# All transposes of a slot between up and down projection, contexts in the work banks, and the second exponentials of the last pair behind silu

## The chip, the cores and the metric

The kernel runs on one core of one Trainium2 chip. The metric is the device time in microseconds (us) of one execution. PE is TensorE, PEld its weight loads, ACT ScalarE, DVE VectorE, POOL GpSimd and SP SyncE, which issues nearly all DMAs here. A time such as "1479.32" is counted in us from the start of the profiled span.

## The reference, cut to what matters

128 graphs of 128 nodes with 384 features go through one transformer layer, with a final layer norm. The bias `adj` is added to the attention scores of all eight heads (48 features each).

```python
q, k, v = (split_heads(x @ w + b) for w, b in ((wq, bq), (wk, bk), (wv, bv)))
scores = einsum('bhqd,bhkd->bhqk', q, k) * 48 ** -0.5 + adj[:, None]
ctx = merge_heads(einsum('bhij,bhjd->bhid', softmax(scores), v))
x1 = rmsnorm(x + ctx @ wo + bo, alpha1, gamma1)
ff = silu(x1 @ w1 + b1) @ w2 + b2            # 384 -> 1536 -> 384
y = rmsnorm(x1 + ff, alpha2, gamma2)
out = layernorm(x + y)
```

## The kernel before

Two graphs make a pair (`PAIR` = 2, index `b`), so there are 64 pairs `g`, the last being 63. One pass of the outer loop is a slot `t`; there are 67 in use. A slot works on several pairs at once: it projects pair `t` to queries, keys and values, takes scores and softmax of pair `t-1`, context and attention output of pair `t-2`, and the feed-forward of pair `t-3`. From slot 3 to slot 63 all of it is live. Each engine has a program of its own, written out by hand in the order of `slot_program(t)`; engines meet through semaphores only, and a wait holds up everything behind it on its engine.

Every product with weights is made of three fp32r passes: each operand is split into a high part (written by ACT, `transposed_hi`, `context_hi`) and a low part (written by DVE, `transposed_lo`, `context_lo`). Products need their input with features on the partitions, so PE transposes `x` (`transpose_x`: 6 matmuls with the identity), the normalised `x1` (`transpose_x1`: 6) and the probabilities (`transpose_probs`: 8 for each graph). ACT copies the transposed probabilities back to SBUF (`probsT_out`, L657), and `context` (L510 and L514, 32-column tiles of the array) reads the copy.

PSUM is full: `ps_att[0]` and `ps_att[1]` (two banks each) hold scores and transposed probabilities, `ps_rows[0]` and `ps_rows[1]` hold contexts, attention outputs and down projections, and `ps_work[0]` and `ps_work[1]` hold the outputs of query, key, value and up projections in turn. The transposes of x and x1 borrow a work bank and a rows bank.

PE's order in a full slot is: transposes of x(t), of the probabilities of graph 0, of x1(t-3), of the probabilities of graph 1; contexts of graph 0 and 1; scores (L526); output product; query, key and value projections; up (six parts of 18 matmuls, L448, each followed by a silu on ACT, L722, and `split_h` on DVE, L883 and L885); down (L595, 36 matmuls for each graph). The transposes thus stand right before the contexts that read them.

ACT does Exp and Silu from different tables and loads each once a slot (L776 and L784). DVE's order around the softmax is: bias and maximum, `residual1`, `norm1` of both graphs (L873 and L877), `keys_out` (L845), `normalise` and `values_out`. SP issues in a slot, among others, the load of x for the residual, the bias, the next x, ten moves of queries and keys within SBUF (L364), and in slot 2 six loads of weights (L324). The first slots also split weights on ACT (L642) and DVE (L802).

Of the kernel before, what the change touches and what calls it, by code (L numbers as in the profile page):

```python
# [26 lines left out]
def build_layer(nc, x, adj, wq, bq, wk, bk, wv, bv, wo, bo, w1, b1, w2, b2,  # L27
# [17 lines left out]
    with ctx:  # L45
# [232 lines left out]
        def x1_first(g):  # L278

            return ps_work[0][:, 0:2 * toks] if g < last else ps_att[0][:, 0:2 * toks]  # L280

        def x1_third(g):

            return ps_rows[1][:, 0:toks] if g < last else ps_att[0][:, 2 * toks:3 * toks]
# [156 lines left out]
        def _(pe):  # L441
# [17 lines left out]
            def transpose_x(g):  # L459
                pe.wait_ge(x_in_loaded, through(g, 16))  # L460

                if live(g - LAG_FF - 1):
                    pe.wait_ge(silu_ready[fc // 2 - 2], through(g - LAG_FF - 1))
                elif live(g - 1):
                    pe.wait_ge(v_ready[0], through(g - 1))
                transpose_rows(ps_work[1][:, 0:2 * toks], x_in, (0, 1), xT_done[0])

                if live(g - LAG_FF - 1):
                    pe.wait_ge(res2_ready[0], through(g - LAG_FF - 1))
                elif live(g - LAG_ATTN - 1):  # L470
                    pe.wait_ge(res1_ready[0], through(g - LAG_ATTN - 1))
                transpose_rows(ps_rows[0][:, 0:toks], x_in, (2,), xT_done[1])

            def transpose_probs(g, b):
                pe.wait_ge(probs_ready[b], through(g, 2))
                for head in range(HEADS):
                    mm = pe.transpose(ps_att[b][:, head * P:(head + 1) * P], probs[:, b, head, :], ident[:])  # L477
                mm.then_inc(probsT_done[b], 1)

            def transpose_x1(g):  # L480
                for b in range(PAIR):
                    pe.wait_ge(x1_ready[b], through(g))

                if g == last:
                    pe.wait_ge(probsT_ready[0], through(g))
                elif live(g - 1):
                    pe.wait_ge(res2_ready[1], through(g - 1))
                transpose_rows(x1_third(g), x1[:, g % 2], (2,), x1T_done[1])

                if g < last:  # L490
                    if live(g - 1):
                        pe.wait_ge(silu_ready[fc // 2 - 1], through(g - 1))
                    else:
                        pe.wait_ge(v_ready[1], through(g + LAG_FF - 1))
                transpose_rows(x1_first(g), x1[:, g % 2], (0, 1), x1T_done[0])

            def context(g, b):
                pe.wait_ge(probsT_ready[b], through(g))
                pe.wait_ge(v_ready[b], through(g))

                if b == 0 and live(g + LAG_ATTN):
                    pe.wait_ge(xT_lo[1], through(g + LAG_ATTN))
                elif b == 0:
                    pe.wait_ge(res2_ready[0], through(g + LAG_ATTN - LAG_FF - 1))
                elif live(g + LAG_ATTN - LAG_FF):
                    pe.wait_ge(x1T_lo[1], through(g + LAG_ATTN - LAG_FF))
                for side in range(2):
                    for pair in range(hp):
                        head = 2 * pair + side
                        pe.matmul(ps_rows[b][pair * TILE:(pair + 1) * TILE, 2 * P:3 * P], v_rest[:, g % 2, b, head, :],  # L510
                                  probs[:, b, place(head), :], start=(side == 0), stop=(side == 1))
                for head in range(HEADS):
                    p0, at = head % 4 * TILE, head // 4 * P
                    mm = pe.matmul(ps_rows[b][p0:p0 + TILE, at:at + P], v_first[:, g % 2, b, head, :],  # L514
                                   probs[:, b, place(head), :], start=True, stop=True)
                mm.then_inc(ctx_done[b], 1)

            def scores(g, b):
                if b == 0:
                    pe.wait_ge(qk_moved, through(g, 16 * len(moves)))  # L520
                if live(g - 1):
                    pe.wait_ge(probsT_ready[b], through(g - 1))
                for head in range(HEADS):
# [8 lines left out]
            def output_product(g, b):  # L532
                pe.wait_ge(ctx_lo[b], through(g))
# [4 lines left out]
            def project_qk(g):  # L538
                for i in range(2):
                    pe.wait_ge(xT_lo[i], through(g))  # L540
                for n, blocks in enumerate((((wq_s, 0), (wq_s, 1)), ((wq_s, 2), (wk_s, 0)),
# [4 lines left out]
                    if n == 0 and live(g - LAG_FF):  # L546
                        pe.wait_ge(x1T_lo[0], through(g - LAG_FF))
                    elif n == 0 and live(g - 1):
                        pe.wait_ge(v_ready[1], through(g - 1))
                    elif n == 2:  # L550
                        pe.wait_ge(qk_ready[0], through(g))
# [14 lines left out]
            def up(g):  # L566
# [3 lines left out]
                for m in range(fc // 2):  # L570
# [5 lines left out]
                    elif m == 0 or g == last:  # L576
# [22 lines left out]
            def slot_program(t):  # L599
                g_scores, g_attn, g_ff = t - LAG_SCORES, t - LAG_ATTN, t - LAG_FF  # L600
                if live(t):
                    transpose_x(t)
                if live(g_attn):
                    transpose_probs(g_attn, 0)
                if live(g_ff) and g_ff < last:
                    transpose_x1(g_ff)
                if live(g_attn):
                    transpose_probs(g_attn, 1)
# [14 lines left out]
                if live(g_ff):  # L623
# [3 lines left out]
                    if g_ff == last - 1:  # L627
                        transpose_x1(last)
# [8 lines left out]
        def _(act):  # L637
# [22 lines left out]
            def context_hi(g, b):  # L660
                act.wait_ge(ctx_done[b], through(g))
                act.activation(ctxT[:, b, HI].rearrange("p c n -> p (c n)"), ps_rows[b][:, 0:d],
# [65 lines left out]
            def slot_program(t):  # L728
                g_scores, g_attn, g_ff, g_out = t - LAG_SCORES, t - LAG_ATTN, t - LAG_FF, t - LAG_FF - 1
                if t == 0:  # L730
                    weights_hi(t, "queries")
                if live(t):
                    transposed_hi(t, 0, ps_work[1], xT_done, xT, xT_hi)
                    transposed_hi(t, 1, ps_rows[0], xT_done, xT, xT_hi)
                if t == 0:
                    weights_hi(t, "keys")
                    weights_hi(t, "values")
                if live(g_attn):
                    probsT_out(g_attn, 0)
                if live(g_ff) and g_ff < last:  # L740
                    transposed_hi(g_ff, 1, x1_third(g_ff), x1T_done, x1T, x1T_hi)
                if live(g_attn):
                    probsT_out(g_attn, 1)
                    context_hi(g_attn, 0)
                if live(g_ff) and g_ff < last:
                    transposed_hi(g_ff, 0, x1_first(g_ff), x1T_done, x1T, x1T_hi)
                if live(g_attn):
                    context_hi(g_attn, 1)
                if live(g_out):
                    output_squares(g_out, 1)  # L750
                weights_hi(t, "softmax")
# [15 lines left out]
                if live(g_scores):  # L767
# [6 lines left out]
                weights_hi(t, "end")  # L774
                if live(g_ff):
# [4 lines left out]
                    if g_ff == last - 1:  # L780
                        transposed_hi(last, 1, x1_third(last), x1T_done, x1T, x1T_hi)
                        transposed_hi(last, 0, x1_first(last), x1T_done, x1T, x1T_hi)
                    if live(g_scores + 1):
                        act.preload_act_table(ACT.Exp)  # L784
                    output_squares(g_ff, 0)
# [4 lines left out]
        def _(dve):  # L790
# [21 lines left out]
            def context_lo(g, b):  # L812
                dve.wait_ge(ctx_hi[b], through(g))
                dve.tensor_tensor(ctxT[:, b, LO].rearrange("p c n -> p (c n)"), ps_rows[b][:, 0:d],  # L814
# [101 lines left out]
            def slot_program(t):  # L916
# [5 lines left out]
                if live(t):  # L922
                    transposed_lo(t, 0, ps_work[1], xT_hi, xT, xT_lo)
                    transposed_lo(t, 1, ps_rows[0], xT_hi, xT, xT_lo)
                if t == 0:
# [3 lines left out]
                if live(g_ff) and g_ff < last:  # L929
                    transposed_lo(g_ff, 1, x1_third(g_ff), x1T_hi, x1T, x1T_lo)  # L930
                if live(g_attn):
                    context_lo(g_attn, 0)
                if live(g_ff) and g_ff < last:
                    transposed_lo(g_ff, 0, x1_first(g_ff), x1T_hi, x1T, x1T_lo)
                if live(g_attn):
                    context_lo(g_attn, 1)
# [30 lines left out]
                if live(g_scores):  # L967
                    for half in range(2):
                        normalise(g_scores, 1, half)
                weights_lo(t, "end")  # L970
                if live(g_ff):
# [3 lines left out]
                    if g_ff == last - 1:  # L975
                        transposed_lo(last, 1, x1_third(last), x1T_hi, x1T, x1T_lo)
                        transposed_lo(last, 0, x1_first(last), x1T_hi, x1T, x1T_lo)
# [31 lines left out]
```

## Time and profile before

| | |
|---|---|
| time, median of 3 runs | 2948.49 us (2948.18 to 2950.1) |
| the profiled execution | 2949.07 us, its span 2947.3 us |
| granted TensorE clock, mean | 0.997 of full speed |
| PE busy | 2910.8 us, 99% of the span |
| PEld busy | 2857.1 us, 97% |
| DVE, ACT, POOL busy | 63%, 49%, 23% |
| one full slot, from transposes to transposes | 45.43 us |

In the timeline a row is a run of like instructions on one engine: start, length, engine, line, operation, output and input tiles, and count. Matmuls overlap: a row's length runs to the end of its last one, so the pace of matmuls is read from starts. A bracket at the end is idle time of the engine and what ended it.

### The profile page before, as it was taken

What the parts mean: (1) busy time and instruction counts of PE and PEld (TensorE: products, weight loads), DVE (VectorE), ACT (ScalarE), POOL (GpSimd) and SP (SyncE); (2) the same over time, 40 slices, a digit from 0 to 9 for tenths busy, and PEclk for the clock granted to TensorE, in tenths of its full rate; (3) what the DMA queues carried; (4) which work ended last, traced back from release to release, by engine and by line L of the source; (5) the groups of instructions that cost most, each with busy time, mean ns of one, the idle gap of its engine ahead of it and who ended that gap; (6) DMA issues with size and microseconds to landing.
All of it is one profiled execution on the core that took longest, in us unless ns stands there. A gap on an engine that the chain in (4) does not pass through costs nothing.

```text
span 2947.3 us, 62438 instructions
## 1 busy us (share of the span) xinstructions
PE 2910.8 (99%) x25216; PEld 2857.1 (97%) x25216; DVE 1853.1 (63%) x3621; ACT 1443.2 (49%) x4258; POOL 684.8 (23%) x968
## 2 busy tenths in 40 slices
PE   7999999999999999999999999999999999999998
PEld 7999999999999999999999999999999999999998
DVE  6665656657666566566665665656656656566564
ACT  5544545545445455454454554544545445445442
POOL 0122222222222222222222222222221222222222
PEclk9999999999999999999999999999999999999999
DMA  5211212212112121121221211212212112122110
GB/s 164 80 51 53 69 40 64 57 52 64 48 56 69 40 64 56 54 64 44 60 64 46 64 53 52 68 42 62 61 48 64 53 51 69 41 63 60 49 46 28
DMA packets 155489, 171.91 MB, mean 58 GB/s; under 512 B 18624, under 2 KB 155200, under 8 KB 155200
## 3 DMA queue, kind: packets, MB, share of 16 engines
q1 hardware_dynamic: 151952, 166.92, 19.5%
q8 instruction: 199, 3.26, 0.5%
q10 hardware_dynamic: 3248, 0.99, 0.2%
q14 instruction: 90, 0.74, 0.1%
HBM read 92.35 MB, written 25.17 MB: 40 GB/s over the span
## 4 chain that ended last, share of the span: by engine, by line
PE 95%; ACT 3%; DVE 1%; DMA 1%; SPq 1%; issue 0%; POOL 0%; ACTq 0%; POOLq 0%
PE ps_work L448 47%; PE ps_rows L595 28%; PE ps_rows L448 7%; PE ps_att L526 4%; PE ps_att L477 4%; ACT probs L657 2%; PE ps_work L456 2%; PE ps_rows L510 1%; PE ps_rows L514 1%; PE ps_rows L456 1%; SPq L364 0%; DMA x_in<-in_x 0%; ACT probs L668 0%; DVE w_s L802 0%; DMA stage<-in_L_gnn_wq 0%
## 5 line engine op out<-in xcount | busy, mean ns | idle before, releaser
L448 PE MATMUL ps_work<-x1T,w_s 128*128 128x256 f32 x6912 | 823.2, 280 | 3.7 <-ACT h_raw L722 3.7
L448 PEld LDWEIGHTS ps_work<-x1T,w_s 128*128 128x128 f32 x6912 | 820.8, 188 | 3.9 <-ACT h_raw L722 3.9
L595 PE MATMUL ps_rows<-w_s,h 128*128 128x384 f32 x4608 | 824.0, 340 | 0.0
L595 PEld LDWEIGHTS ps_rows<-w_s,h 128*128 128x128 f32 x4608 | 810.6, 188 | 0.0
L722 ACT ACTIVATE h_raw<-ps_work,b_col 128x256 f32<-128x256 f32 x768 | 322.3, 471 | 534.8 <-PE ps_work L448 531.3
L668 ACT ACTIVATE probs<-probs,neg_max 128x128 f32<-128x128 f32 x1024 | 396.4, 390 | 158.2 <-DVE neg_max L827 158.2
L430 POOL TENSOR_TENSOR x<-x,rows 128x768 f32<-128x768 f32 x64 | 117.7, 1840 | 1165.4 <-DVE h L885 1165.4
L883 DVE CAST h<-h_raw 128x512 fp32r<-128x512 f32 x384 | 164.3, 428 | 313.8 <-ACT h_raw L722 313.8
L894 DVE TENSOR_TENSOR y<-ps_rows,x 128x384 f32<-128x384 f32 x128 | 71.4, 558 | 415.0 <-PE ps_rows L595 415.0
L885 DVE TENSOR_TENSOR h<-h_raw,h 128x512 fp32r<-128x512 f32 x384 | 265.9, 692 | 13.2
L697 ACT ACTIVATE squares<-y 128x384 f32<-128x384 f32 x128 | 66.6, 521 | 329.3 <-DVE y L894 329.3
L448 PE MATMUL ps_work<-xT,wq_s 128*128 128x256 f32 x1728 | 216.9, 283 | 2.8 <-DVE xT L809 2.8
L448 PE MATMUL ps_rows<-wo_s,ctxT 128*128 128x384 f32 x1152 | 217.8, 343 | 0.0
L448 PEld LDWEIGHTS ps_work<-xT,wq_s 128*128 128x128 f32 x1728 | 214.5, 191 | 3.4 <-DVE xT L809 3.1
L448 PE MATMUL ps_work<-wv_s,xT 128*128 128x384 f32 x1152 | 211.6, 337 | 4.0 <-DVE qk_flat L845 3.0
L448 PE MATMUL ps_work<-xT,wk_s 128*128 128x256 f32 x1728 | 213.4, 280 | 0.9 <-ACT qk_flat L706 0.9
L448 PEld LDWEIGHTS ps_work<-xT,wk_s 128*128 128x128 f32 x1728 | 207.4, 188 | 1.1 <-ACT qk_flat L706 1.1
L448 PEld LDWEIGHTS ps_rows<-wo_s,ctxT 128*128 128x128 f32 x1152 | 197.3, 188 | 7.9 <-DVE ctxT L814 0.3
L418 POOL TENSOR_TENSOR x_in<-x_in,rows 128x768 f32<-128x768 f32 x64 | 117.0, 1828 | 374.3 <-DMA x_in<-in_x 374.3
L448 PEld LDWEIGHTS ps_work<-wv_s,xT 128*128 128x128 f32 x1152 | 197.6, 188 | 5.0 <-DVE qk_flat L845 3.6
L652 ACT ACTIVATE xT<-ps_work 128x512 fp32r<-128x512 f32 x64 | 38.2, 597 | 333.1 <-PE ps_work L456 333.1
L668 ACT ACTIVATION_READ_ACCUMULATOR probs<-probs,neg_max 128x1 f32 x1024 | 193.1, 189 | 0.0
(87 smaller groups left out, 3576.8 us busy)
## 6 DMA issues: line engine op xcount, KB each, us to landing
x_in<-in_x SPq DMA_DIRECT2D x128, 384.0 KB, 3.1
qk<-qk_flat SPq DMA_DIRECT2D x381, 96.0 KB, 2.3
x_last<-in_x SPq DMA_DIRECT2D x64, 384.0 KB, 3.6
out<-y SPq DMA_DIRECT2D x63, 384.0 KB, 2.7
bias<-in_adj SPq DMA_DIRECT2D x64, 128.0 KB, 2.1
qk<-qk_flat SPq DMA_DIRECT2D x127, 64.0 KB, 2.1
qk<-qk_flat SPq DMA_DIRECT2D x127, 32.0 KB, 2.0
stage<-in_L_gnn_w SPq DMA_DIRECT2D x17, 192.0 KB, 4.0
```

The costliest lines, as they stand in the source:

```text
L418: pool.tensor_tensor(x_in[:], x_in[:], row(BO), ALU.add).then_inc(x_res_biased, 1)
L430: pool.tensor_tensor(x1[:, g_ff % 2], x1[:, g_ff % 2], row(B2), ALU.add).then_inc(x1_b2_ready, 1)
L448: mm = pe.matmul(ps_out, stationary(sta), moving(mov), start=(i == 0), stop=(i == n - 1))
L456: mm = pe.transpose(ps_out[:, at:at + P], rows_in[:, b, kb * P:(kb + 1) * P], ident[:])
L477: mm = pe.transpose(ps_att[b][:, head * P:(head + 1) * P], probs[:, b, head, :], ident[:])
L526: mm = pe.matmul(ps_att[b][:, at:at + P], qk[p0:p0 + dh, Q, c, b * P:(b + 1) * P], qk[p0:p0 + dh, K, c, b * P:(b + 1) * P], start=True, st ...
L595: mm = pe.matmul(ps_rows[b][:, 0:d], h[:, sta, m, b * P:(b + 1) * P], w2_s[:, mov, m, :], start=(m == 0 and i == 0), stop=(m == fc - 1 and ...
L668: e = act.activation(probs[:, b, head, :], probs[:, b, head, :], ACT.Exp, bias=neg_max[:, b, head:head + 1], accum_out=row_sum[:, b, head: ...
L722: e = act.activation(h_raw[:, m % 2, j * toks:(j + 1) * toks], ps_work[(m + 1) % 2][:, j * toks:(j + 1) * toks], ACT.Silu, bias=b1_col[:, ...
L883: dve.tensor_copy(hi, h_raw[:, m % 2, :]).then_inc(h_hi[m], 1)
L885: dve.tensor_tensor(h[:, LO, 2 * m:2 * m + 2, :].rearrange("p c n -> p (c n)"), h_raw[:, m % 2, :], hi.bitcast(F32), ALU.subtract).then_in ...
L894: dve.tensor_tensor(y[:, b, :], ps_rows[b][:, 0:d], x1[:, g % 2, b, :], ALU.add).then_inc(res2_ready[b], 1)
```

## The change

In a full slot PE now begins with both contexts; scores, output product, projections and up follow as before. Between up and down stand all transposes: probabilities of pair `t-1` (both graphs), x of pair `t+1`, x1 of pair `t-2`, each one slot earlier than it was. The contexts lie in `ps_work[0]` and `ps_work[1]`, the transposes of x in `ps_work[1]` and `ps_work[0]`, those of x1 in `ps_att[0]`, behind ACT's copy out of that tile. ACT and DVE have their copies in the matching places, ahead of the Exp table load. On DVE `norm1` of graph 1 moves behind the layer norm of graph 1, that is, from ahead of `keys_out` to behind `values_out`. For the last pair the probabilities are transposed at the start of slot 65, and the exponentials of its graph 1, with their normalisation, come behind the silus and x1 copies of slot 64.

```diff
 PE
-        def x1_first(g): ... ps_work[0] (last pair: ps_att[0])
-        def x1_third(g): ... ps_rows[1] (last pair: ps_att[0])
+        x_banks = (ps_work[1][:, 0:2 * toks], ps_work[0][:, 0:toks])
+        x1_banks = (ps_att[0][:, 0:2 * toks], ps_att[0][:, 2 * toks:3 * toks])
...
             def transpose_x(g):
+                for i, blocks in enumerate(((0, 1), (2,))):
+                    if live(g - LAG_FF - 1):
+                        pe.wait_ge(silu_ready[fc // 2 - 2 + i], through(g - LAG_FF - 1))
+                    elif live(g - 1):
+                        pe.wait_ge(v_ready[i], through(g - 1))
+                    transpose_rows(x_banks[i], x_in, blocks, xT_done[i])
...
             def transpose_x1(g):
+                if g == last - 1:
+                    pe.wait_ge(scores_biased[0], through(last))
+                else:
+                    pe.wait_ge(probsT_ready[0], through(min(g + 1, last)))
...
             def context(g, b):
                 pe.wait_ge(probsT_ready[b], through(g))
                 pe.wait_ge(v_ready[b], through(g))
+                if live(g + LAG_ATTN):
+                    pe.wait_ge(xT_lo[1 - b], through(g + LAG_ATTN))
-                        pe.matmul(ps_rows[b]...
+                        pe.matmul(ps_work[b]...
...
             def scores(g, b):
+                if b == 0 and live(g + LAG_SCORES - LAG_FF):
+                    for i in range(2):
+                        pe.wait_ge(x1T_lo[i], through(g + LAG_SCORES - LAG_FF))
...
             def slot_program(t):
-                transpose_x(t); transpose_probs(g_attn, 0)
-                transpose_x1(g_ff); transpose_probs(g_attn, 1)
+                if g_attn == last:
+                    for b in range(PAIR):
+                        transpose_probs(last, b)
                 context(g_attn, 0 and 1); scores; output_product; projections; up(g_ff)
+                if live(g_scores) and g_scores < last:
+                    for b in range(PAIR):
+                        transpose_probs(g_scores, b)
+                if live(g_ff) and live(t + 1):
+                    transpose_x(t + 1)
+                if live(g_attn):
+                    transpose_x1(g_attn)
                 down(g_ff, 0 and 1)
 ACT
+                if live(g_out):
+                    output_squares(g_out, 1)        # now ahead of the contexts
+                context_hi(g_attn, 0 and 1)
...
-                if live(g_scores):
+                if live(g_scores) and g_scores < last:
                     exponentials(g_scores, 1)
                 silu(g_ff)
+                probsT_out(g_scores, 0 and 1); x_out(); transposed_hi(g_attn, x1 banks)
+                    if live(g_scores + 1) or g_scores == last:
                         act.preload_act_table(ACT.Exp)
+                    if g_scores == last:
+                        exponentials(last, 1)
 DVE
-                    for b in range(PAIR):
-                        norm1(g_attn, b)
+                    norm1(g_attn, 0)
                 keys_out, normalise, values_out, layer_norm(g_out, 1)
+                if live(g_attn):
+                    norm1(g_attn, 1)
```

## Rows read from the trace of the kernel before

**Rows 1.** The page: busy line of the engines, the chain that ended last by line.
```profile
PE 2910.8 (99%) x25216; PEld 2857.1 (97%) x25216; DVE 1853.1 (63%) x3621; ACT 1443.2 (49%) x4258; POOL 684.8 (23%) x968
...
PE ps_work L448 47%; PE ps_rows L595 28%; PE ps_rows L448 7%; PE ps_att L526 4%; PE ps_att L477 4%; ACT probs L657 2%; PE ps_work L456 2%; PE ps_rows L510 1%; PE ps_rows L514 1%; PE ps_rows L456 1%; SPq L364 0%; DMA x_in<-in_x 0%; ACT probs L668 0%; DVE w_s L802 0%; DMA stage<-in_L_gnn_wq 0%
```

**Rows 2.** All waits: who waited for whom, us in total, times, longest.
```profile
PEld ps_rows L510 <- ACT probs L657: 23.7, 64, 0.4
...
PEld ps_rows L510 <- issue: 10.8, 64, 0.2
...
PE ps_work L448 <- ACT h_raw L722: 3.7, 1, 3.7
```

**Rows 3.** Timeline of PE over one full slot.
```profile
1476.17 0.60 PE L456 MATMUL ps_work<-ident,x_in 128*128 128x128 f32 x4
...
1478.35 1.04 PE L477 MATMUL ps_att<-ident,probs 128*128 128x128 f32 x8
1479.32 0.64 PE L510 MATMUL ps_rows<-probs,v_rest 128*32 128x128 f32 x16
1479.78 0.62 PE L514 MATMUL ps_rows<-probs,v_first 128*32 128x128 f32 x16
1480.50 0.65 PE L510 MATMUL ps_rows<-probs,v_rest 128*32 128x128 f32 x16
...
1481.51 2.06 PE L526 MATMUL ps_att<-qk 48*128 48x128 f32 x32
...
1508.88 12.88 PE L595 MATMUL ps_rows<-w_s,h 128*128 128x384 f32 x72
1521.60 0.60 PE L456 MATMUL ps_work<-ident,x_in 128*128 128x128 f32 x4
```

**Rows 4.** Timeline of PE, second half of the matmuls that begin at 1479.78.
```profile
1479.99 0.40 PE L514 MATMUL ps_rows<-probs,v_first 128*32 128x128 f32 x8
```

**Rows 5.** Timeline of ACT in the same slot: copy, sixth silu, table load.
```profile
1479.42 1.02 ACT L657 ACTIVATE probs<-ps_att 128x1024 f32<-128x1024 f32 x1 [0.23 <-PE ps_att L477]
...
1509.08 0.84 ACT L722 ACTIVATE h_raw<-ps_work,b_col 128x256 f32<-128x256 f32 x2 [1.27 <-PE ps_work L448]
1509.94 1.28 ACT L784 ACT_TABLE_LOAD   x1
```

**Rows 6.** Timeline of PE, slot 65: up, transposes, down.
```profile
2900.64 0.82 PE L456 MATMUL ps_att<-ident,x 128*128 128x128 f32 x6
2901.22 12.73 PE L595 MATMUL ps_rows<-w_s,h 128*128 128x384 f32 x72
```

**Rows 7.** Timeline of ACT in slot 3: a weight's copy, then a silu.
```profile
90.99 0.52 ACT L642 ACTIVATE w_s<-stage 128x384 fp32r<-128x384 f32 x1
92.32 0.84 ACT L722 ACTIVATE h_raw<-ps_work,b_col 128x256 f32<-128x256 f32 x2 [0.80 <-PE ps_work L448]
```

**Rows 8.** Timeline of PE in slot 3, second value projection.
```profile
86.23 1.83 PE L448 MATMUL ps_work<-wv_s,xT 128*128 128x384 f32 x9 [1.69 <-DVE qk_flat L845]
```

**Rows 9.** Timeline of DVE in slot 3.
```profile
77.86 0.56 DVE L868 TENSOR_TENSOR x<-ps_rows,x_in 128x384 f32<-128x384 f32 x1 [4.86 <-POOL x_in L418]
...
84.18 0.61 DVE L873 SCALAR_TENSOR_TENSOR x<-x,inv_rms,rows 128x384 f32<-128x384 f32 x1
...
85.30 0.87 DVE L845 TENSOR_SCALAR qk_flat<-ps_work,bk_col 128x256 f32<-128x256 f32 x2
```

**Rows 10.** Timeline of SP, the residual's load of slot 3.
```profile
71.73 0.38 SPq L315 DMA_DIRECT2D x_in<-in_x  x1
```

**Rows 11.** Timeline of slot 64: PE, ACT and DVE.
```profile
2849.09 4.43 PE L448 MATMUL ps_work<-x1T,w_s 128*128 128x256 f32 x36
2857.25 10.32 PE L448 MATMUL ps_work<-x1T,w_s 128*128 128x256 f32 x72 [3.73 <-ACT h_raw L722]
...
2851.78 0.19 ACT L686 ACTIVATION_READ_ACCUMULATOR squares<-x 128x1 f32 x1
...
2857.26 0.48 DVE L913 TENSOR_SCALAR y<-y,mean_var,inv_std 128x384 f32<-128x384 f32 x1
```

More of the change, by code:

```diff
@@ L482, in transpose_x1 @@
                     pe.wait_ge(x1_ready[b], through(g))
[L484 to L495, printed above, removed]
+                if g == last - 1:
+                    pe.wait_ge(scores_biased[0], through(last))
+                else:
+                    pe.wait_ge(probsT_ready[0], through(min(g + 1, last)))
+                for i, blocks in enumerate(((0, 1), (2,))):
+                    transpose_rows(x1_banks[i], x1[:, g % 2], blocks, x1T_done[i])
             def context(g, b):
@@ L499, in context @@
                 pe.wait_ge(v_ready[b], through(g))
[L501 to L506, printed above, removed]
+                if live(g + LAG_ATTN):
+                    pe.wait_ge(xT_lo[1 - b], through(g + LAG_ATTN))
+                else:
+                    pe.wait_ge(silu_ready[fc // 2 - 1 - b], through(g + LAG_ATTN - LAG_FF - 1))
                 for side in range(2):
@@ L544, in project_qk @@
                         pe.wait_ge(weight_split, (n + 1) * kd)
[L546 to L550, printed above, removed]
+                    if n == 2:
                         pe.wait_ge(qk_ready[0], through(g))
@@ L779, in slot_program @@
                     silu(g_ff)
[L780 to L783, printed above, removed]
+                elif live(t + 1):
+                    x_out()
+                weights_hi(t, "end")
+                if live(g_scores) and g_scores < last:
+                    for b in range(PAIR):
+                        probsT_out(g_scores, b)
+                if live(g_ff) and live(t + 1):
+                    x_out()
+                if live(g_attn):
+                    for i in range(2):
+                        transposed_hi(g_attn, i, x1_banks[i], x1T_done, x1T, x1T_hi)
+                if live(g_ff):
+                    if live(g_scores + 1) or g_scores == last:
                         act.preload_act_table(ACT.Exp)
+                    if g_scores == last:
+                        exponentials(last, 1)
                     output_squares(g_ff, 0)
@@ L928, in slot_program @@
                     weights_lo(t, "values")
-                if live(g_ff) and g_ff < last:
-                    transposed_lo(g_ff, 1, x1_third(g_ff), x1T_hi, x1T, x1T_lo)
                 if live(g_attn):
[L932 to L936, printed above, removed]
+                    for b in range(PAIR):
+                        context_lo(g_attn, b)
                     if g_attn == 0:
@@ L966, in slot_program @@
                     layer_norm(g_out, 1)
-                if live(g_scores):
+                if live(g_attn):
+                    norm1(g_attn, 1)
+                if live(g_scores) and g_scores < last:
                     for half in range(2):
                         normalise(g_scores, 1, half)
-                weights_lo(t, "end")
                 if live(g_ff):
@@ L974, in slot_program @@
                         weights_lo(t, m)
-                    if g_ff == last - 1:
-                        transposed_lo(last, 1, x1_third(last), x1T_hi, x1T, x1T_lo)
-                        transposed_lo(last, 0, x1_first(last), x1T_hi, x1T, x1T_lo)
+                if live(t + 1):
+                    for i in range(2):
+                        transposed_lo(t + 1, i, x_banks[i], xT_hi, xT, xT_lo)
+                weights_lo(t, "end")
+                if live(g_attn):
+                    for i in range(2):
+                        transposed_lo(g_attn, i, x1_banks[i], x1T_hi, x1T, x1T_lo)
+                if g_scores == last:
+                    for half in range(2):
+                        normalise(last, 1, half)
+                if live(g_ff):
                     residual2(g_ff, 0)
```

75 lines of the change are left out of this document (27 added, 48 removed).

## The prediction

> **What bounds the kernel now.** I read the page first. PE is busy for 99% of the span, and the chain that ended last is PE nearly throughout; the one other line with a visible share is ACT's copy of the transposed probabilities, L657, with 2% [rows 1]. No other engine can be the bound of a full slot, so what is there to win is PE's idle time and nothing else, and the list of waits says where that lies. Weight loads of the context's first line wait 64 times for ACT's copy, 23.7 us in total, and 64 times for nothing visible, 10.8 us; and there is one long wait of 3.7 us for a silu [rows 2]. Then the timeline of a full slot, for the exact size. Slots repeat every 1521.60 - 1476.17 = 45.43 us [rows 3]. The transposes of graph 1 begin at 1478.35, the copy of them begins 1.07 us later and takes 1.02 us [rows 5], and the context of graph 1 can only start at 1480.50, when that copy has ended [rows 3]. The context of graph 0 fills part of the time, not all.
>
> **The gap in a full slot.** The second half of the context's 16 matmuls at L514 starts at 1479.99 [rows 4], the first at 1479.78 [rows 3], so eight take 0.21 and 16 take 0.43 us. Context 1 could start at 1480.21; it starts at 1480.50, which is 0.29 us lost. It also starts from an idle array: from L510 to L514 it is 0.46 us in a context that begins so [rows 3], against 0.43 at pace, another 0.02 to 0.03. With both contexts at the head of the slot, copies made a down projection earlier (12.72 us, from 1508.88 to 1521.60), this is gone: **0.31 us a slot**.
>
> **The joints.** The change replaces three joints of PE's order (down to transposes, transposes to context, up to down) by three others (up to transposes, transposes to down, down to context). First the pace of transposes: four run 0.60 us and eight 1.04 us from the first start to the last end [rows 3], so one takes 0.11 us at pace and 0.27 us by itself. Up to transposes to down exists already in slot 65: six transposes begin at 2900.64 and down at 2901.22 [rows 6], 0.58 us where six at pace take 0.65; these two joints cost nothing. Down to context is new. Its nearest row is transposes to context: eight transposes and the joint take 0.97 us [rows 3], some 0.09 us above their pace of 0.88. I take the same for down to context, so the joint nets to nothing: the 10.8 us of "issue" ahead of the contexts [rows 2] stay, only behind another neighbour. The bounds of the new joint are 0 (then another 0.09 us a slot is won) and 0.16 us: a matmul of down has a pace of 12.72 / 72 = 0.177 us and the last runs to 1521.76 [rows 3], so it takes 0.34 us by itself, 0.07 more than a transpose; if that is paid in full, 0.07 us a slot is lost.
>
> The Trainium skill, "TensorEngine Tiling (Array Packing)", section Key Properties, says that changing the tiling mode, not just the tile, drains TensorE. By it the context's 32-column tiles must wait for whatever stood before to leave the array. The trace agrees: the passage from transposes into the context shows 0.09 us [rows 3]. By this rule the number of changes of mode is the same before and after, and only the longer matmul ahead speaks against the change.
>
> **What could be late behind the moved transposes.** Call the end of up U. The 16 transposes of probabilities and 6 of x take 22 x 0.109 = 2.4 us (0.109 is the 0.11 above with a digit more, (1.04 - 0.27) / 7), all 28 with those of x1 take 3.05 us. Those of x need the fifth and sixth silu. The sixth ends at 1509.08 + 0.84 = 1509.92, U + 1.04, as up ends at 1508.88 [rows 3, 5]; the block that needs it comes at U + 2.2. Those of x1 go into `ps_att[0]` and wait for ACT's copy of graph 0: the copy may begin at U + 1.07, just when the silu is done, ends at U + 2.10, and PE follows a copy by 0.05 us (1480.44 to 1480.50) [rows 3, 5]: U + 2.15. PE is there at U + 2.40. This is the tightest place of the new order; **it has 0.25 us to spare**. Behind it on PE stands down, so lateness here counts in full. Down needs only its first high and low parts of h, long done, and the sixth only at its eleventh step. ACT then has copies of graph 1, x and x1 (about 3 us) and the table load of 1.28 us [rows 5] until about U + 6, before squares that wait for the first half of down; DVE's four subtractions end near U + 5.5. All that is covered by down.
>
> At the head of the next slot ACT has squares first, then two context copies. Contexts take 1.8 us and scores 2.0 us [rows 3], so the output product starts about 4.0 us after down's end; down's residual, squares and both splits of context 0 end at about 2.5, of context 1 at 3.2, since each is an operation of 384 columns like that at 77.86, 0.56 us [rows 9]. Cost 0; without this cover it would be as much as they come late. DVE's `norm1` of graph 1 (85.30 - 84.18 = 1.12 us [rows 9]) moves behind the value outputs and delays the first split of h by under 1 us, against 1.5 us until the third silu asks for it: cost 0. On SP the residual's load now waits for transposes one slot earlier, so it lands during down; what stands behind it (bias, next x) is not wanted before the middle of the next slot. POOL adds to it behind its work for graph 0 and is done about 0.7 us into the slot, before the root that it owes graph 1. The extra waits before scores and the output product are for things 10 us old.
>
> **How many slots.** Contexts stand in slots 2 to 65. In slots 2 and 3 PE waits for DVE's normalised probabilities or for a DMA right there, so nothing is won; slot 65 is below. Slots 4 to 64 are 61: 61 x 0.31 = **18.9 us**.
>
> **The first slots.** In slot 3 the second value projection waits 1.69 us for `keys_out` [rows 8], which stands behind both `norm1` on DVE. One of them moves away: 1.12 us earlier [rows 9]. The chain ahead of it hangs on the residual's load, issued at 71.73 [rows 10]; in SP's order it stands behind six weight loads and ten moves, which start when `keys_out` of slot 2 is done; that has the same `norm1` ahead of it, so it too is about 1.15 us earlier, and so is DVE's residual at 77.86, which waited 4.86 us for it [rows 9]. Together 1.12 + 1.15 = **2.3 us**, bounds 0 and 2.6. Slots 1 and 2 win and lose a few tenths, since DVE's order ends at the same time; I take 0.
>
> **The last slots.** In slot 64 the third part of up waits for silu. ACT is free of squares at 2851.97 [rows 11] and had the eight exponentials of graph 1 next; without them the table is loaded until 2853.25 and the first silu ends at 2854.1. PE began at 2849.09 and its two parts run 4.43 us to the last end [rows 11], so with 0.17 us of overlap the third could start at 2853.35: 0.8 us idle, and 2.1 us for a part. The third silu then waits for the first split of h, which DVE reaches after its layer norm (2857.26 + 0.4) [rows 11] and has done at 2858.75 (estimated at 1.1 us, as the two operations of `norm1` [rows 9]); the silu ends at 2859.6, and PE, which had the fourth part done at 2858.4, idles 1.25. In all 2.05 us against 3.9 before (from 2853.35 to 2857.25): **1.8 us** won, bounds 1.2 and 3.7. The exponentials end about 8 us behind up, under down. In slot 65 both transposes of probabilities now stand bare ahead of the contexts: 0.31 for the first copy and 0.14 for the second, against 0.31 before: 0.14 lost.
>
> **Sum.** 18.9 + 2.3 + 1.8 - 0.1 = 22.9 us. The profiled execution took 2949.07 (span 2947.3): 2926.2. The median of the runs is 0.6 lower: **2925.6 us**.
>
> **Rivals.**
> 1. *The longer matmul makes down to context dear*, 0.07 us a slot: 61 x 0.07 = 4.3 less, 2929.9. For it: the last matmul of down is longer. Against: it is also longer at pace (0.177 against 0.109). 0.12.
> 2. *Only the full slots win*, because the first slots hang on something else (weights) and slot 64 on DVE: 18.9 alone, 2929.6. For it: DVE and SP are both crowded there. 0.08.
> 3. *The stall moves to the transposes of x1.* If the copy of graph 0 ends 0.25 us later than worked out, PE starts to wait; at 0.25 + 0.31 = 0.56 us the full slots win nothing, and only the ends (4 us) or less remain: 2944 to 2948. For it: ACT has silu and copy back to back. Against: both durations stand in the rows to 0.02 us. 0.05.
> 4. *Slower: the copies stand between Silu and Exp, and each change of function loads a table.* One more load of 1.28 us ahead of the copy at U + 1.07 makes the x1 transposes 1.28 - 0.25 = 1.03 us late. From 0.56 us on it decides the sign. 61 x (1.03 - 0.31) = 44 slower, less 4: 2989. Against it: in slot 3 copies of weights stand between silus, with 0.80 us idle between copy and next silu, and no load [rows 7]. Any other lateness of ACT at this place over 0.56 us belongs here too. 0.07.
>
> The Trainium skill, "ScalarE: Activation LUTs", section Table sets, says that tables are loaded as sets of functions, one load for each change of set. By it a copy could cost a load at this place if it were not in silu's set; in this trace it is.
>
> **How the numbers follow.** Forecast 0.68, rivals 0.12, 0.08, 0.05 and 0.07. Range: up to rivals 1 and 2 with a part of both together, 2933; down, if the new joint costs nothing (61 x 0.09 = 5.5) with 0.5 for the ends: 2920. Forecast alone: 2923 to 2928. No change that can be told is within 0.2%, 5.9 us: 2942.6 to 2954.4. Faster by more: 0.88; within: 0.05; slower: 0.07.
>
> **What would show it.** The L510 wait for ACT's copy should vanish from the list but for slot 65; a slot should take 45.12 us; context 0 should follow down by some 0.27 us from the last matmul's start, and context 1 follow at pace; up should be followed by 28 transposes in 3.05 us without a hole; the value projection of slot 3 should wait under 1 us. A wait of PE at L456 for L657 would be rivals 3 or 4, with an added table load in the latter; a longer hole ahead of L510 rival 1.

## The result, and the profile after

The changed kernel takes 2911.72 us (median of 4 runs, 2910.08 to 2916.1), the one before 2949.3 (4 runs beside it): ratio 0.9876, 95% interval 0.9861 to 0.9891. That is 37.6 us less, where 22.9 were forecast (2925.6) and the range ended at 2920. The direction was right, the size was not.

The page after has a span of 2908.3 us, 39.0 below the 2947.3 of before. Its busy line and its chain answer to [rows 1]:

```profile
PE 2882.5 (99%) x25216; PEld 2841.8 (98%) x25216; DVE 1846.2 (63%) x3621; ACT 1431.3 (49%) x4259; POOL 684.3 (24%) x968
...
PE ps_work L443 48%; PE ps_rows L581 27%; PE ps_rows L443 7%; PE ps_att L514 4%; PE ps_att L470 4%; PE ps_work L495 2%; PE ps_work L499 2%; PE ps_att L451 1%; PE ps_work L451 1%; SPq L359 0%; DMA x_in<-in_x 0%; DVE w_s L802 0%; DMA stage<-in_L_gnn_wq 0%; POOL x_in L413 0%; DVE neg_max L827 0%
```

ACT's copy, 2% of the chain before, is gone from it. But look at PE: the same 25216 matmuls are busy for 2882.5 us instead of 2910.8, 28.3 us less. A closed gap explains part of that, because the profile counts the drain of the last matmul before a gap as busy: of the 0.31 us that the gap cost, 0.10 were idle (1479.78 + 0.62 = 1480.40 to 1480.50 [rows 3]). The other 0.21 in 61 slots are 13 us, less than half of the 28.3. The rest has to lie elsewhere. The waits of the changed kernel (answer to [rows 2]) show the gap closed and the joint left:

```profile
PEld ps_work L495 <- issue: 15.7, 63, 0.3
...
PEld ps_work L495 <- ACT probs L649: 0.8, 2, 0.5
```

And one full slot on PE, which answers to [rows 3] and [rows 6]:

```profile
1459.16 0.64 PE L495 MATMUL ps_work<-probs,v_rest 128*32 128x128 f32 x16
1459.62 0.62 PE L499 MATMUL ps_work<-probs,v_first 128*32 128x128 f32 x16
1460.06 0.62 PE L495 MATMUL ps_work<-probs,v_rest 128*32 128x128 f32 x16
...
1475.75 12.83 PE L443 MATMUL ps_work<-x1T,w_s 128*128 128x256 f32 x108
1488.42 1.91 PE L470 MATMUL ps_att<-ident,probs 128*128 128x128 f32 x16
1490.17 0.82 PE L451 MATMUL ps_work<-ident,x_in 128*128 128x128 f32 x6
1490.82 0.82 PE L451 MATMUL ps_att<-ident,x 128*128 128x128 f32 x6
1491.39 12.73 PE L581 MATMUL ps_rows<-w_s,h 128*128 128x384 f32 x72
1504.06 0.65 PE L495 MATMUL ps_work<-probs,v_rest 128*32 128x128 f32 x16
```

Context 1 follows context 0 after 0.44 us from L499 to L495, at pace; the transposes run without a hole. The slot takes 1504.06 - 1459.16 = 44.90 us against 45.43: 0.53 less, not 0.31. The missing 0.22 is in down. Its 72 matmuls run 12.73 us here and 12.88 before [rows 3], although the one here begins with a slower first step (0.26 us). Ten microseconds from the middle of down, before and then after:

```profile
1509.77 10.41 PE L595 MATMUL ps_rows<-w_s,h 128*128 128x384 f32 x58
```

```profile
1492.69 10.56 PE L581 MATMUL ps_rows<-w_s,h 128*128 128x384 f32 x60
```

A stretch of n matmuls lasts n-1 steps and the 0.34 us of the last one: (10.41 - 0.34) / 57 = 0.1767 us a step before, (10.56 - 0.34) / 59 = 0.1732 after. Over 70 steps that is 0.24 us a slot, in matmuls with the same operands and shapes, all at a granted clock of 1.00. In the slow pace the steps alternate between 0.179 and 0.174 us, in the quick one each is 0.173. The same difference stands already in the rows of before: 12.88 us for down in a usual slot [rows 3], 12.73 in slot 65, where six transposes stand ahead of it [rows 6]. And it stands the other way round in the changed kernel's slot 66, the only one in which down still follows up directly:

```profile
2887.47 12.88 PE L581 MATMUL ps_rows<-w_s,h 128*128 128x384 f32 x72
```

### The profile page after: what moved, and what is told of

The parts are those of the page before. It is cut to its first block, busy times and chain, and to the rows that moved or that the text cites. A ratio compares the mean times of both kernels' runs of the same rounds, so it can differ in the third digit from the quotient of the medians.

```text
span 2908.3 us, 62626 instructions
## 1 busy us (share of the span) xinstructions
PE 2882.5 (99%) x25216; PEld 2841.8 (98%) x25216; DVE 1846.2 (63%) x3621; ACT 1431.3 (49%) x4259; POOL 684.3 (24%) x968
## 4 chain that ended last, share of the span: by engine, by line
PE 97%; DVE 1%; DMA 1%; SPq 1%; ACT 0%; issue 0%; POOL 0%; ACTq 0%; POOLq 0%; DVEq 0%
PE ps_work L443 48%; PE ps_rows L581 27%; PE ps_rows L443 7%; PE ps_att L514 4%; PE ps_att L470 4%; PE ps_work L495 2%; PE ps_work L499 2%; PE ps_att L451 1%; PE ps_work L451 1%; SPq L359 0%; DMA x_in<-in_x 0%; DVE w_s L802 0%; DMA stage<-in_L_gnn_wq 0%; POOL x_in L413 0%; DVE neg_max L827 0%
## 5 line engine op out<-in xcount | busy, mean ns | idle before, releaser
L581 PE MATMUL ps_rows<-w_s,h 128*128 128x384 f32 x4608 | 815.0, 337 | 0.0
L581 PEld LDWEIGHTS ps_rows<-w_s,h 128*128 128x128 f32 x4608 | 796.2, 188 | 0.0
L391 POOL TENSOR_SCALAR mean_sq<-sum_sq 128x1 f32<-128x1 f32 x256 | 53.8, 210 | 816.8 <-ACT squares L678 467.0
L835 DVE TENSOR_TENSOR probs<-probs,row_inv 128x512 f32<-128x512 f32 x256 | 177.9, 695 | 8.7
```

The lines of the kernel that those rows point to most:

```text
L581: mm = pe.matmul(ps_rows[b][:, 0:d], h[:, sta, m, b * P:(b + 1) * P], w2_s[:, mov, m, :], start=(m == 0 and i == 0), stop=(m == fc - 1 and ...
L835: dve.tensor_tensor(probs[:, b, heads], probs[:, b, heads], row_inv[:, b, heads].unsqueeze(2).to_broadcast([P, hp, P]), ALU.mult).then_inc ...
```

## The experiments

**1. One transpose more, in the kernel before.** Theory A says that down's pace is set by what enters the array ahead of it, theory B that other engines or banks beside it set it.

```diff
+            def tick(g):
+                if live(g):
+                    pe.wait_ge(scores_biased[0], through(g))
+                pe.transpose(ps_att[0][:, 0:P], ident[:], ident[:])
...
                     if g_ff == last - 1:
                         transpose_x1(last)
+                    else:
+                        tick(g_scores)
                     for b in range(PAIR):
                         down(g_ff, b)
```

> The kernel before with one identity transpose more, into a free bank, between up and down. Theory A (the pace of down's 72 matmuls is set by what enters the array directly ahead of them): down runs at 0.173 us a matmul instead of 0.177 in the slots that had the slower pace, 0.22 to 0.24 us a slot less; the transpose itself and its joint cost about 0.11; the slot takes 45.31 to 45.33 us, the time 2942 (7 us below before). Theory B (down is faster after the change because other engines or other banks are busy beside it): down stays at 0.177, the slot takes 45.54 us, the time 2956.

Measured: 2942.22 us (7 runs), ratio to before 0.9974, interval 0.9963 to 0.9985. One superfluous instruction a slot makes the kernel 7.8 us faster than its own runs of before (2950.05). Its slot is 1504.73 - 1459.43 = 45.30 us:

```profile
1459.43 0.27 PE L602 MATMUL ps_att<-ident 128*128 128x128 f32 x1
1459.46 12.73 PE L595 MATMUL ps_rows<-w_s,h 128*128 128x384 f32 x72
...
1504.73 0.27 PE L602 MATMUL ps_att<-ident 128*128 128x128 f32 x1
```

Down takes 12.73 us with nothing else of the change made. Theory B falls. Down starts only 0.03 us after the transpose; its first step then takes 0.26 us instead of 0.18, so the transpose costs about 0.11 in all and gives back 0.24.

**2. All transposes between the halves of down, in the changed kernel.**

```diff
+                if live(g_ff):
+                    down(g_ff, 0)
                 if live(g_scores) and g_scores < last:
...
                 if live(g_ff):
-                    for b in range(PAIR):
-                        down(g_ff, b)
+                    down(g_ff, 1)
```

> The changed kernel with all transposes between the two halves of down, so that the first half stands directly behind up. Theory A: the first 36 matmuls at 0.177, the other 36 at 0.173, slot 45.0 us against 44.90, time 2918 to 2919. Theory B: both halves at 0.173, slot 44.9, time as the changed kernel, 2911 to 2912. In both the context's gap stays closed.

Measured: 2922.35 us (4 runs), ratio to before 0.9903 (0.9887 to 0.9918); slot 1539.46 - 1494.44 = 45.02 us.

```profile
1494.44 6.52 PE L581 MATMUL ps_rows<-w_s,h 128*128 128x384 f32 x36
1500.79 1.91 PE L470 MATMUL ps_att<-ident,probs 128*128 128x128 f32 x16
...
1503.77 6.50 PE L581 MATMUL ps_rows<-w_s,h 128*128 128x384 f32 x36
```

The first half is at the slow pace, (6.52 - 0.34) / 35 = 0.1766; the second, after its first step of 0.26, at (6.50 - 0.34 - 0.26) / 34 = 0.1735. Within one slot and one kernel the pace changes at the transposes. The slot fits theory A; the total is 3 to 4 us above it, and slot 65 has nearly all of that. There the output product waits 2.19 us for DVE, whose work now comes late (0.48 in the changed kernel), and then takes 4.88 us instead of 3.36, because the granted clock is 0.50 from 2857.2 to 2860.6.

```profile
2857.33 4.88 PE L443 MATMUL ps_rows<-wo_s,ctxT 128*128 128x384 f32 x18 [2.19 <-DVE ctxT L815]
```

**3. One matmul of up's own kind instead of the transpose, in the kernel before.** The tick is `pe.matmul(ps_att[0][:, 0:toks], x1T[:, HI, 0, 0:P], x1T[:, HI, 0, :])`.

> The kernel before with one fp32r matmul of 128x256 more (the kind that up is made of) between up and down, in place of the transpose of the first experiment. Theory A1 (it is the kind of instruction ahead of down that counts): down stays at 0.177, slot 45.43 + 0.12 = 45.55 us, time 2956. Theory A2 (it is the phase at which down enters the stream, whatever stands ahead): one step more shifts the phase, and down may run at 0.173, slot 45.3 to 45.35, time about 2942 to 2944.

Measured: 2954.88 us (one run), slot 1511.17 - 1465.63 = 45.54 us. Ten microseconds of down:

```profile
1466.82 10.41 PE L595 MATMUL ps_rows<-w_s,h 128*128 128x384 f32 x58
```

Again 58 in 10.41 us, the slow pace. In slots 3 to 63 the matmul changes nothing, as A1 has it. In slot 64 down was quick before and is quick here. But in slot 66, where up itself follows down directly, down was slow before and is quick here. Down of slot 66, before and then here:

```profile
2926.46 12.88 PE L595 MATMUL ps_rows<-w_s,h 128*128 128x384 f32 x72
```

```profile
2932.48 12.65 PE L595 MATMUL ps_rows<-w_s,h 128*128 128x384 f32 x72
```

So one matmul of up's own kind can turn the pace too, and A1, by which it can't, does not hold everywhere. What stands further back counts as well.

**4. A pause between up and down, in the kernel before.**

```diff
-                    if b == 0 and m % 2 == 0:
-                        pe.wait_ge(h_lo[m // 2], through(g))
+                    if b == 0 and m == 0:
+                        for part in range(fc // 2):
+                            pe.wait_ge(h_lo[part], through(g))
```

> The kernel before, where down waits for all six parts of h before its first matmul, so PE stands idle some 2.3 us between up and down in every slot. Time 2948 + 64 x 2.3 = about 3095. The pace of down is what is asked: A1 (kind of instruction) 0.177, since up is still the last thing ahead; A2 (phase, reset by a break) 0.173, and the slot 0.2 us below 45.43 + 2.3.

Measured: 3103.07 us (one run).

```profile
1490.14 12.74 PE L596 MATMUL ps_rows<-w_s,h 128*128 128x384 f32 x72 [2.21 <-DVE h L886]
```

Down is quick behind a pause as well, with up still the last thing ahead. So it is not the transpose as such. The total is 8 us above the expected 3095. In six full slots the granted clock falls to 0.50 for 3.4 us while down runs (14.17 us instead of 12.74 for the down that begins at 390.05), 1.4 to 1.7 us each.

**5. Probabilities transposed at the head of every slot, in the changed kernel.** The conditions `g_attn == last` become `live(g_attn)` and the transposes of `g_scores` go; x and x1 stay between up and down.

> The changed kernel, but the probabilities of every pair are transposed at the head of the slot, right before the contexts that read them, as the changed kernel does for the last pair; x and x1 stay between up and down. If the closed gap is worth 0.31 us and the quick down comes from any transpose ahead of it: down stays at 0.173, context 0 waits for ACT's copy as in slot 65 of the changed kernel (2.15 us from the first transpose to the context, 0.31 to 0.33 us of it lost), slot 45.21 to 45.25 us against 44.90, time 2911.7 + 61 x 0.33 = about 2932. Rival (down is quick only behind all 28 transposes, or the copies beside it matter): down at 0.177, slot 45.45, time about 2946.

Measured: 2976.61 us (4 runs), ratio to before 1.0096 (1.0079 to 1.0113): slower than both, and neither theory's number. Slot 1494.45 - 1448.51 = 45.94 us.

```profile
1448.51 1.91 PE L470 MATMUL ps_att<-ident,probs 128*128 128x128 f32 x16
1450.65 0.65 PE L495 MATMUL ps_work<-probs,v_rest 128*32 128x128 f32 x16 [0.24 <-ACT probs L646]
...
1479.94 0.60 PE L451 MATMUL ps_work<-ident,x_in 128*128 128x128 f32 x4
1481.03 0.44 PE L451 MATMUL ps_work<-ident,x_in 128*128 128x128 f32 x2 [0.49 <-ACT h_raw L711]
...
1481.88 12.73 PE L581 MATMUL ps_rows<-w_s,h 128*128 128x384 f32 x72
```

The context waits as forecast: 2.14 us from the first transpose, with 0.24 idle. Down is quick behind x and x1 alone. What the expectation left out is the sixth silu: the last block of x may only be written when it is done, at U + 1.09, and without the 16 transposes ahead PE is there at U + 0.43. That is 0.65 us a slot. 0.33 + 0.65 = 0.98 of the 1.04 us by which the slot grew.

**6. Both `norm1` ahead of the keys again, in the changed kernel.**

> The changed kernel with the second norm1 back ahead of the keys on DVE. If the first slots won 3.8 us through it: the value projection of slot 3 waits about 1.5 us again instead of 0.35, slot 2 hands its moves on 1.1 us later, up of slot 3 begins 2.3 us later than 84.06, full slots stay at 44.90, time 2914. Rival (the first slots won by other things, such as the context's banks or a warmer start): up of slot 3 begins at 84 to 84.5, time 2912.

Measured: 2913.55 us (one run). The value projections of slots 2 and 3:

```profile
60.76 1.83 PE L443 MATMUL ps_work<-wv_s,xT 128*128 128x384 f32 x9 [1.28 <-DVE qk_flat L845]
...
85.87 1.83 PE L443 MATMUL ps_work<-wv_s,xT 128*128 128x384 f32 x9 [1.70 <-DVE qk_flat L845]
```

Both stalls are back; with the move the one of slot 3 is 0.35 us, as these rows of the changed kernel show:

```profile
38.68 0.60 PE L451 MATMUL ps_work<-ident,x_in 128*128 128x128 f32 x4
...
82.39 1.83 PE L443 MATMUL ps_work<-wv_s,xT 128*128 128x384 f32 x9 [0.35 <-DVE qk_flat L845]
84.06 12.83 PE L443 MATMUL ps_work<-x1T,w_s 128*128 128x256 f32 x108
```

From the transposes of x(2) to up of slot 3 the changed kernel takes 84.06 - 38.68 = 45.38 us. The kernel before took 47.57 (87.89 - 40.32), this experiment 47.13 (87.54 - 40.41, where 87.54 is 85.87 and the 1.67 us that the row at 82.39 lasts before up begins). So the move of `norm1` is worth 1.75 of the 2.2 us that the first slots won, each read from one execution. The changed kernel's execution has 3.4 us at a granted clock of 0.50 within it (from 63.5), which the two others have not; experiment 8, whose first slots are in the same order, has none there either and takes 86.17 - 41.08 = 45.09 us, so this costs about 0.3 us. The stretch ahead differs by 1.6 us between the profiled executions of before and after, but executions of the same order differ there as much (38.68, 40.19 in the next experiment, and 40.41 here). The granted clock explains it: near the start it is 0.50 for 6.8 us before (from 24.3) and in these two experiments, and for 3.4 us after (from 26.0), which is 1.7 us of work. So it isn't put down to the change.

**7. The last pair's second exponentials ahead of silu again, in the changed kernel.**

> The changed kernel with the last pair's second exponentials and their normalisation ahead of silu again. The stall of slot 64 was 3.9 us before and 2.3 after: expected 3.9 us between the second and the third part of up, up of slot 64 longer by 1.6 to 1.8 us, nothing else, time 2913.5. Rival (the shorter stall came from the transposes that left the slot's head): up as in the changed kernel.

Measured: 2914.8 us (one run). Slot 64 here, then in the changed kernel:

```profile
2814.35 4.39 PE L443 MATMUL ps_work<-x1T,w_s 128*128 128x256 f32 x36
2822.54 10.33 PE L443 MATMUL ps_work<-x1T,w_s 128*128 128x256 f32 x72 [3.80 <-ACT h_raw L714]
2832.71 0.82 PE L451 MATMUL ps_att<-ident,x 128*128 128x128 f32 x6
```

```profile
2812.94 4.39 PE L443 MATMUL ps_work<-x1T,w_s 128*128 128x256 f32 x36
2818.06 4.54 PE L443 MATMUL ps_work<-x1T,w_s 128*128 128x256 f32 x36 [0.72 <-ACT h_raw L714]
2823.67 4.50 PE L443 MATMUL ps_work<-x1T,w_s 128*128 128x256 f32 x36 [1.07 <-ACT h_raw L714]
2828.00 0.82 PE L451 MATMUL ps_att<-ident,x 128*128 128x128 f32 x6
```

Up takes 18.36 us here and 15.06 in the changed kernel, where 12.67 is its length without stalls: the part is worth 3.3 us, not 1.6 to 1.8. The bracket of 3.80 is one part of it. The other is in the row behind it, where 72 matmuls take 10.33 us and should take 8.6. These 1.7 us are no hidden stall: PE is busy all through, but its granted clock is 0.50 from 2823.1 to 2826.5. The kernel before has the same in its slot 64. A row of this view gives the stretch, its length, the busy time of PE, PEld, DVE, ACT and POOL, the granted clock, the share of DMA and GB/s:

```profile
2857.40:2860.80 3.40, 3.40 (x17) 3.40 (x18) 3.26 (x9) 0.53 (x2) 0.00 (x0) 0.50 0.60 174
```

In the changed kernel the clock is 1.00 throughout this up. All runs agree: where slot 64 has one stall of 3.7 to 3.8 us (before and experiments 1, 3, 4, 7 and 9) the clock falls to 0.50 right around its end, for 3.4 or 6.8 us, and where it has two of 0.6 to 1.1 us (after and experiments 2, 5, 6 and 8) the clock stays. So the stalls differ by 1.6 us, as expected, and 1.7 are the clock, which the expectation left out.

**8. One transpose ahead of up, in the changed kernel** (`tick` before `up`).

> The changed kernel with one identity transpose more, into a free bank, between the value projection and up. Asked: has up, with its 108 matmuls of 256 columns at a mean of 0.1174 us, a quicker pace too when it is entered through a transpose, as down has? If so by as much as down (2 per cent, 0.2 us or more), the slot takes 44.75 to 44.8 us and the time is 2903 to 2906. If up has one pace only, the slot takes 44.90 + 0.03 to 0.11 and the time is 2914 to 2919. I hold the second for likelier, since the parts of up after the breaks of slot 64 run no quicker than the others.

Measured: 2927.98 us (4 runs), ratio to before 0.9932 (0.9917 to 0.9947); slot 1485.96 - 1440.80 = 45.16 us.

```profile
1440.80 0.27 PE L588 MATMUL ps_att<-ident 128*128 128x128 f32 x1
1440.82 13.07 PE L443 MATMUL ps_work<-x1T,w_s 128*128 128x256 f32 x108
...
1485.96 0.27 PE L588 MATMUL ps_att<-ident 128*128 128x128 f32 x1
```

Both expectations missed: up became slower, 13.07 us against 12.83. Ten microseconds of up, before and then here:

```profile
1497.74 10.49 PE L448 MATMUL ps_work<-x1T,w_s 128*128 128x256 f32 x88
```

```profile
1486.79 10.48 PE L443 MATMUL ps_work<-x1T,w_s 128*128 128x256 f32 x87
```

A matmul of 256 columns takes 0.28 us by itself, so a step is (10.49 - 0.28) / 87 = 0.1174 us before and (10.48 - 0.28) / 86 = 0.1186 here. Up has two paces too, but behind the transpose it runs at the slow one. Slot 3 is an exception: there up has the transpose ahead and still runs at 0.1174; the value projection before it is broken by waits, which may be why.

**9. The same ahead of up in the kernel before, where down follows up directly.**

> The kernel before with one identity transpose more between the value projection and up; down stands directly behind up. The eighth experiment showed up at 0.1188 us a matmul behind such a transpose, instead of 0.1174, 0.26 us a slot with the transpose itself. Theory P (each stage keeps the phase with which it is entered, and up's slow phase hands over to down's quick one, as in slot 64 of the kernel before, where up had been broken and down ran at 0.1733): down runs at 0.173 though up is right ahead of it, slot 45.43 + 0.26 - 0.23 = 45.46 us, time 2948 to 2951. Theory N (it is the neighbour that counts: right behind up, down is slow): down at 0.1767, slot 45.69 us, time 2965.

Measured: 2951.46 us (10 runs), ratio to before 1.001 (1.0 to 1.0019). Slot 1496.80 - 1451.34 = 45.46 us.

```profile
1451.34 0.27 PE L602 MATMUL ps_att<-ident 128*128 128x128 f32 x1
1451.37 13.07 PE L448 MATMUL ps_work<-x1T,w_s 128*128 128x256 f32 x108
1464.27 12.65 PE L595 MATMUL ps_rows<-w_s,h 128*128 128x384 f32 x72
...
1496.80 0.27 PE L602 MATMUL ps_att<-ident 128*128 128x128 f32 x1
```

Ten microseconds of down here:

```profile
1464.80 10.39 PE L595 MATMUL ps_rows<-w_s,h 128*128 128x384 f32 x59
```

(10.39 - 0.34) / 58 = 0.1733. Down is quick with up right ahead of it, so theory N falls: a transpose 109 matmuls back decides down's pace, and something is carried through the whole of up. Of theory P this first half holds. Its second half, that it is up's slow pace that hands over to a quick down, does not. In slot 3 of this run up is behind the transpose and runs at 0.1174, and down behind it is quick:

```profile
87.72 12.92 PE L448 MATMUL ps_work<-x1T,w_s 128*128 128x256 f32 x108
100.48 12.65 PE L595 MATMUL ps_rows<-w_s,h 128*128 128x384 f32 x72
```

Ten microseconds of that up:

```profile
89.80 10.37 PE L448 MATMUL ps_work<-x1T,w_s 128*128 128x256 f32 x87
```

(10.37 - 0.28) / 86 = 0.1173. Slot 64 is alike: the last third of up at 0.1174, down at 0.1733. In the kernel before 62 ups at 0.1174 stand ahead of a slow down. So up's pace does not tell which pace down will have.

## Why the prediction was wrong

**The step that failed** is in "The joints". The prediction took 12.72 us for down as a constant ("a matmul of down has a pace of 12.72 / 72 = 0.177 us") and asked only what the joints around it cost. The change altered the pace: 0.1732 us a matmul instead of 0.1767, 0.24 us less a slot. Experiments 1 and 2 show that this comes from the transposes ahead of down and from nothing else of the change. The evidence was in the prediction's own rows, 12.88 us for a usual down [rows 3] and 12.73 behind transposes [rows 6]; from the second row it read the start of down (0.58 us for six transposes) and not its length. With 0.22 us for 61 slots, 13 to 14 us, the forecast would have been 2912, and the measured median is 2911.72. That they meet so closely is in part luck, as the last slots were off by another 1.3 us.

**The gap: right.** Context 1 follows at pace, 0.31 us a slot. Experiment 5 brings the wait back and shows it.

**The joints: right in sum, not each.** Down to context costs what was taken: "issue" rose from 10.8 us (64 times) [rows 2] to 15.7 (63 times), 0.25 us instead of 0.17, but a step of down is itself 0.06 longer than one of transposes. Transposes to down costs less at its start (0.03 us where 0.11 was pace) and as much more in down's first step. Rival 1, the dearer drain of a longer matmul, did not come; what the Trainium skill's "TensorEngine Tiling (Array Packing)", section Key Properties, says of changes of mode held for the joints (0.27 us from the last matmul of down to the context, 0.09 above down's pace, as it was 0.09 above the pace of transposes before [rows 3]); it says nothing of the pace behind them.

**What might be late: right.** ACT's first copy did end in time: in slots 3 to 62 PE never waits at L451 for it. Two idle times of 0.2 to 0.3 us behind copies are left: in slot 63, which has no transposes of a next x ahead of those of x1, and in slot 65. No table load came with the copies: L649 starts 0.03 us after the sixth silu in the trace after, and rival 4 falls. Experiment 5 shows that the order had a second tight place that the prediction passed as safe because 16 transposes stand before it.

**The first slots: right.** 2.3 us forecast, 2.2 measured over slots 2 and 3.

**The last slots: mis-sized.** 1.8 us forecast for slot 64, 3.3 measured (up took 2867.41 - 2849.09 = 18.32 us before, 15.06 after), inside the bounds given. The stall was sized well: the 2.05 us left were right within 0.3 us. What the prediction put at nothing is the clock: 1.7 us of the row of 72 matmuls [rows 11] were lost because the granted clock fell to 0.50 for 3.4 us behind the long stall, and with the shorter stalls it didn't fall (experiment 7). Slot 65 lost more than the 0.14 us forecast: its output product waits 0.48 us for DVE.

**The sum as measured.** From up of slot 3 to up of slot 63 the trace is 32.2 us shorter (60 slots at 0.54), slots 2 and 3 give 2.2, slots 63 to 65 give 3.0, and 1.6 are the start, which varies from one execution to the next with the clock there (experiment 6): 39.0.

No version tried beats the changed kernel. The experiments point to one more place, the down of slot 66: experiment 1 has a transpose ahead of it, and from up of slot 66 to the end takes 33.4 us instead of 33.5. That is far below what the time of a run can tell, and it wasn't tried in the changed kernel.

## What to carry to other kernels

On a kernel whose TensorE is never idle, compare the length of a stage of matmuls in all its occurrences before taking it as a constant: two lengths for one stage mean that its pace can be moved. Read a stage's length against count times pace too, and where it is longer, look at the granted clock of that stretch before looking for stalls: behind a stall of 3.8 us it cost another 1.7 here. Where a step is moved, ask of each thing that it stood before what that was waiting for: the mover may have been its cover (experiment 5, 0.65 us a slot).

## What the runs showed of the hardware

A long run of equal matmuls has more than one steady pace and, without a break in it, keeps the one in which it is entered. All at a granted clock of 1.00, with 128x128 weights in fp32r loaded for each matmul:

| | matmuls of 384 columns (down) | of 256 columns (up) |
|---|---|---|
| directly behind the stage before, full slots of before | 0.1767 us | 0.1174 us |
| entered through an fp32 transpose | 0.1733 us | 0.1186 us, but 0.1174 in slot 3 |
| entered after a pause of 2.2 us | 0.1733 us | not measured by itself |
| down directly behind an up that was entered through a transpose (experiment 9) | 0.1733 us | |
| down behind one more matmul of up's kind (experiment 3) | 0.1767 us, but 0.1733 in slot 66 | |

For down the first is from 62 of its 64 occurrences before, and holds for all 72 matmuls, 12.5 us long; the two others are quick, slot 64 behind an up broken by a stall and slot 65 behind transposes. One and the same instruction thus costs 0.11 us and gives 0.24 ahead of down (experiment 1), and costs 0.26 in all ahead of up (experiment 8). Neither the instruction right ahead nor the pace of the stage ahead is enough to tell which pace follows: down was quick and slow behind ups of the same 0.1174, and the transpose did not slow the up of slot 3. What in TensorE holds the states apart no run here tells; that stays open, so a second pace is found by trying and not by rule.

The granted clock fell to 0.50 (1.2 GHz) around the end of the stall of 3.7 to 3.8 us in slot 64, in each of the six runs that have it, and in none of the five in which PE stood for 0.6 to 1.1 us at a time there. Behind waits of 2.2 us it fell in some cases only: in slot 65 of experiment 2 and in six of the 61 full slots of experiment 4. In the kernel before, 3.4 us at this level with PE busy throughout cost 1.7 us.
